# The copy of a value product's result, one slot earlier at the end of each attention layer

## The reference

```python
# layer 0: 16 query heads, 8 key/value heads of 128, RMS norm and rotation of q and k, window of 128
probs = softmax(where(mask, (q * scale) @ k.T, lowest))
x = x + einsum('btnh,nhd->btd', probs @ v, out_kernel)
x = x + sparse_2_of_4(silu(h @ w_gate) * (h @ w_up)) @ w_down    # h = layernorm(x)
# layer 1: 16 heads of 128, causal
z = softmax(masked / sqrt(128)) @ v
x = x + einsum('df,bqf->bqd', W_O, z_flat)
x = x + fwht(silu(h @ W1.T) * (h @ W3.T)) @ W2.T
```

## Time and profile before

| what | us |
|---|---|
| time, median of 3 runs | 709.01 (708.73 to 710.05) |
| the profiled execution: time | 709.12 |
| its span, first to last instruction | 707.3 |
| TensorE busy | 692.6 (98%) |
| VectorE busy | 541.0 (76%) |
| ScalarE busy | 453.3 (64%) |
| GpSimd busy | 359.5 (51%) |
| mean granted TensorE clock | 0.998 |
| layer 0, slots 60 to 63 (TensorE) | 254.44 to 264.23 |
| layer 0, slots 64 to 67 to the last output but one | 264.23 to 278.21 |
| layer 1, slots 60 to 63 | 614.81 to 623.48 |
| layer 1, slots behind 63 up to the first gate product | 623.48 to 635.78 |

### The profile page before, as it was taken

One profiled execution on the slowest core, in us unless ns is written; L12 is line 12 of the kernel. 1 busy time (PEld: TensorE's weight loads), 2 busy tenths in 40 slices (PEclk: granted clock), 3 DMA queues, 4 the chain that ended last, 5 costly groups with the idle time before them and its releaser, 6 DMA issues.

```text
span 707.3 us, 16400 instructions
## 1 busy us (share of the span) xinstructions
PE 692.6 (98%) x4540; PEld 625.4 (88%) x4540; DVE 541.0 (76%) x1696; ACT 453.3 (64%) x1794; POOL 359.5 (51%) x557
## 2 busy tenths in 40 slices
PE   6999999999999998999999999999999999999998
PEld 3789999999999997888878999999999999977887
DVE  5879999999899988969845667766767777796443
ACT  3888888888888885423257666666666666664221
POOL 5998898898899844002069842323232323016100
PEclk9999999999999999999999999999999999999999
DMA  7010210101021010100021010101001100000000
GB/s 237 2 46 9 98 46 2 46 0 44 1 104 60 0 75 2 45 1 0 16 90 61 1 61 1 61 6 54 21 38 41 63 0 0 1 1 0 1 31 31
DMA packets 9178, 24.78 MB, mean 35 GB/s; under 512 B 928, under 2 KB 3232, under 8 KB 8992
## 3 DMA queue, kind: packets, MB, share of 16 engines
q1 hardware_dynamic: 8688, 23.27, 9.7%
q10 hardware_dynamic: 432, 0.85, 0.3%
HBM read 23.07 MB, written 1.05 MB: 34 GB/s over the span
## 4 chain that ended last, share of the span: by engine, by line
PE 87%; DVE 5%; issue 3%; ACT 3%; DMA 1%; POOL 1%; SPq 0%; ACTq 0%; DVEq 0%; POOLq 0%
PE bank L508 12%; PE bank L889 11%; PE bank L500 11%; PE bank L398 11%; PE bank L527 7%; PE bank L412 5%; PE bank L366 5%; PE bank L430 5%; PE bank L359 4%; PE bank L435 3%; PE bank L963 3%; PE bank L450 3%; PE bank L967 2%; DVE x L658 1%; PE bank L983 1%
## 5 line engine op out<-in xcount | busy, mean ns | idle before, releaser
L658 DVE SCALAR_TENSOR_TENSOR x<-bank,rinv,x 128x256 f32<-128x256 f32 x256 | 123.1, 481 | 25.0 <-PE bank L398 22.8
L636 ACT ACTIVATE probs<-scores,negmax 128x128 f32<-128x128 f32 (+1 forms) x256 | 117.4, 470 | 9.3 <-DVE negmax L696 7.8
L544 ACT CAST turned<-bank 128x256 fp32r<-128x256 f32 x104 | 38.8, 373 | 101.9 <-PE bank L412 97.6
L774 POOL TENSOR_TENSOR a_hi<-raw_a,zero 128x384 fp32r<-128x384 f32 (+1 forms) x60 | 43.6, 726 | 84.6 <-PE bank L527 84.6
L669 DVE TENSOR_TENSOR enc_lo<-bank,enc_hi 128x256 fp32r<-128x256 f32 x128 | 54.2, 423 | 30.8 <-PE bank L366 21.0
L302 POOL TENSOR_TENSOR ln_r<-ln_ve,neg_half 128x1 f32<-128x1 f32 x26 | 17.0, 654 | 118.8 <-DVE ln_ve L276 118.8
L677 DVE TENSOR_TENSOR turned<-bank,turned 128x256 fp32r<-128x256 f32 x104 | 43.7, 420 | 40.4 <-ACT probs_t L545 40.4
L398 PE MATMUL bank<-b_hi,enc_hi 128*128 128x256 f32 x256 | 73.4, 287 | 0.0
L398 PE MATMUL bank<-b_lo,enc_hi 128*128 128x256 f32 x256 | 72.3, 283 | 0.0
L398 PE MATMUL bank<-b_hi,enc_lo 128*128 128x256 f32 x256 | 72.3, 282 | 0.0
L792 POOL TENSOR_TENSOR rot_a<-rot_a,rot_b 128x384 f32<-128x384 f32 x64 | 64.7, 1011 | 8.5 <-DVE rot_b L764 7.3
(11 more groups left out here) (179 smaller groups left out, 2397.3 us busy)
## 6 DMA issues: line engine op xcount, KB each, us to landing
raw_a<-in_wa SPq DMA_DIRECT2D x10, 768.0 KB, 4.4
raw_a<-in_wa SPq DMA_DIRECT2D x9, 512.0 KB, 4.0
raw_b<-in_wb SPq DMA_DIRECT2D x16, 256.0 KB, 2.7
hid_last<-in_wax SPq DMA_DIRECT2D x2, 512.0 KB, 4.5
w_a<-in_w2t SPq DMA_DIRECT2D x1, 1024.0 KB, 4.9
raw_b<-in_wdown SPq DMA_DIRECT2D x2, 512.0 KB, 3.4
x<-in_x SPq DMA_DIRECT2D x3, 256.0 KB, 4.6
raw_a<-in_wa ACTq DMA_DIRECT2D x1, 512.0 KB, 3.8
```

The lines of the kernel that those rows point to most:

```text
L636: nc.scalar.activation(probs[:, c % 4, c0:c1], scores[:, c % 2, c0:c1], ACT.Exp, bias=negmax[:, c % 2, r:r + 1], scale=-1.0, accum_out=row ...
L658: nc.vector.scalar_tensor_tensor(out=x[:, m % 8, :], in0=output_bank(m)[:, hh * D:(hh + 1) * D], scalar=rinv[:, u, r:r + 1], in1=x[:, m % ...
```

## The change

It touches three places. First, the copy `enc_hi` leaves the body of `act_slot` for a function `act_encoded(m)`. Up to slot 60 it is called as before, with m = c - 4. From slot 60 on it is called with m = c - 3, behind the copy of the turned probabilities and ahead of the exponentials; so slot 60 does both units 56 and 57, and each later one the unit whose value product TensorE does in that slot. This holds for `act_slot` in layer 0's drain too. Second, in VectorE's slots 61 to 63, the remainder `enc_lo` of unit c - 4 comes ahead of the first half of the residual, where it stood between the halves. Third, the same in `tail(t)` for t > 0 of VectorE (layer 1's slots 64 to 70). `dve_drain0` is unchanged: there the remainder was first already.

```diff
--- before.py
+++ after.py
@@ -546,18 +546,23 @@
                 else:
                     nc.scalar.copy(probs_t[:, m % 2, :], bank[PT_BANK][:, 0:384]).then_inc(s["ptev"], 1)
 
-        def act_slot(act, L, it, c):
+        def act_encoded(act, L, it, m):
+
             s = at[L]
-            if c <= TAIL_SLOT:
-                act_turned(act, L, it, c - 3)
-
-            m = c - 4
             if live(it, m):
                 u = m % 8
                 b, hh = u // 2, u % 2
                 need(act, s["pv"], it, m + 1)
                 need(act, s["op"], it, m - hh - 6)
                 nc.scalar.copy(enc[0][:, hh, b * D:(b + 1) * D], bank[O_BANK][:, 0:D]).then_inc(s["ehi"], 1)
+
+        def act_slot(act, L, it, c):
+            s = at[L]
+            if c <= TAIL_SLOT:
+                act_turned(act, L, it, c - 3)
+
+            if c <= TAIL_SLOT:
+                act_encoded(act, L, it, c - 4)
             m = c + 4
             if live(it, m):
                 t = m % 8
@@ -629,6 +634,7 @@
                 act_late_hi(act, c - UNITS + 2)
             if c >= TAIL_SLOT:
                 act_turned(act, L, it, c - 2)
+                act_encoded(act, L, it, c - 3)
             if live(it, c):
                 need(act, s["pt"], it, c - 3)
                 for r, (c0, c1) in enumerate(((0, 128), (128, 384))):
@@ -724,8 +730,11 @@
             else:
 
                 if c < UNITS:
+                    if c > TAIL_SLOT:
+                        dve_enc_lo(dve, L, it, c)
                     dve_residual(dve, L, it, c, 0)
-                    dve_enc_lo(dve, L, it, c)
+                    if c == TAIL_SLOT:
+                        dve_enc_lo(dve, L, it, c)
                     dve_heads_lo(dve, L, it, c)
                     dve_residual(dve, L, it, c, 1)
                     dve_scores_wait(dve, L, it, c)
@@ -1651,8 +1660,8 @@
                     if t < 0:
                         return
                     if t > 0:
+                        dve_enc_lo(dve, L, None, c)
                         dve_residual(dve, L, None, c, 0)
-                        dve_enc_lo(dve, L, None, c)
                         dve_residual(dve, L, None, c, 1)
                         ln_dve_scale(dve, st, t - 1)
                     dve.wait_ge(at[L]["opadd"], UNITS - 8 + t + 1)
```

## The result

The changed kernel takes 713.98 us (median of 5 runs, 712.82 to 714.29) against 709.01 us (708.73 to 710.05): ratio 1.0063, 95% interval 1.0052 to 1.0073. It is slower, by 5.0 us where 2.8 were forecast. The profiled execution took 714.29 us, its span is 712.5.

What follows compares the result with a forecast made beforehand. It took TensorE's product list plus gaps as the bound: hand-overs in layer 0's drain, nearly full VectorE in layer 1's tail. Layer 0 +1.6 and layer 1 +1.2 made +2.8 on 709.12, so 711.9 us, range 709.9 to 713.3.

Steps and rivals of the forecast that it cites:

- Gain ahead of value product 62 in layer 0: Layer 0 from slot 60: earlier copies and remainders shorten TensorE's waits, so product 62 starts 1.0 us earlier.
- First ring: Layer 0: product 62, its copy, `xT_hi` 0, `xT_lo` 0, `xn`, transposition 1 wait in turn; 2.7 us, was 1.46.
- idle time: Layer 0's drain: TensorE idle about 1.9 us ahead of transposition 1, where it was 0.65, and the same at the next.
- Layer 0 without the clock: Layer 0's net loss from both rings after the gain ahead of them: +1.6 us, with no clock effect included.
- Exponentials at no cost: Slots 60 on, both layers: ScalarE's exponentials start 0.2 to 0.9 us later, costed at nothing.
- Layer 1: Layer 1's tail: late `xT_hi` copies and VectorE's new order together cost +1.2 us, reaching TensorE in full.
- `xT_lo` 0 and 1: Layer 1's tail: these VectorE steps, waiting for late `xT_hi` copies, come 0.8 and 1.1 us later.
- VectorE's order: Residual halves side by side cost 0.13 us a slot, hidden by VectorE's idle time or waits; 0.1 in layer 1's slot 67.
- the ring: Both layers: `xT_hi` behind a copy waiting for a value product makes three engines wait in turn; both rings close, chance 0.66.
- the gain in layer 1: Layer 1, wait at 625.18: remainder of result 60 ahead of half a residual starts that value product 0.4 us earlier.
- rival (d): Layer 0's drain: gaps of about 1.9 us lower TensorE's clock, +1.0 us or more, 713.2 us; chance 0.06.
- the drain of before has gaps too and stays at 1.00: Argument against the clock falling in layer 0's drain: the kernel before has gaps there and keeps full clock.

Runs made afterwards that it cites:

- e3: Changed kernel plus eight unused matmuls in each of the two long TensorE gaps of layer 0's drain, ahead of transpositions 1 and 2; 712.73 us.
- e1: Changed kernel with ScalarE's order of before from slot 64 on, the changed one in slots 60 to 63; VectorE's order stays changed; 708.32 us.
- e6: e1 with VectorE in the order of before; 707.75 us.
- e2: Changed kernel with VectorE's three hunks undone, so only ScalarE's part of the change remains; 713.65 us.
- e8: Changed kernel with extra unused matmuls in only the second long gap of layer 0's drain, ahead of transposition 2; 712.96 us.
- e7: Changed kernel with extra unused matmuls in only the first long gap of layer 0's drain, ahead of transposition 1; 713.36 us.
- e4: Kernel before with only VectorE's part of the change; ScalarE as before; 712.87 us.
- e9: Changed kernel with VectorE's layer 0 drain reordered in slots 65 and 66: both residual halves and `xn` ahead of `xT_lo`; 710.31 us.
- e5: Kernel before with the change to ScalarE and VectorE applied only in layer 1; 710.67 us.

## Why the prediction was wrong

Up to the clock, the mechanism held step by step. Gain ahead of value product 62 in layer 0: forecast -1.0, after 267.68 - 254.59 = 13.09 from slot 60 where it was 14.04, so -0.95. First ring: transposition 1 forecast 2.7 us after product 62's start, it is 2.72; idle time forecast 1.9, it is 1.91 and 2.00. Layer 0 without the clock: forecast +1.6, e3 +1.61. Exponentials at no cost: e1 and e6 bear it out. Layer 1: forecast +1.2, measured +1.40. The sizes inside it fit too: `xT_lo` 0 and 1 are 0.86 and 1.25 us later from slot 60 than before (forecast 0.8 and 1.1), value product 62 is 0.40 earlier (forecast 0.4). How much belongs to which part depends on the order in which one adds them. From e6 (-0.51 against before), VectorE's order adds 0.97 (e1) and the ring then 0.94; the other way round the ring adds 2.07 (e2) and VectorE's order then takes 0.16 off. With the ring closed VectorE has waits that hide the order (1.24 and 0.70 us for `xT_hi` 0 and 1 in e2, 0.59 and 0.19 in the changed kernel), as the prediction said. One reason in it doesn't hold: it put the gain in layer 1 down to the remainder that moves ahead of half a residual, but e6 and e2, which leave VectorE's order alone, have value product 61 0.50 us earlier from slot 60 than before, the changed kernel 0.39.

The step that failed is rival (d), "the gaps of about 1.9 us in layer 0 slow TensorE". I gave it a chance of 0.06 and a price of 1.0 us, and the sum put the clock at nothing. It is what happened in the profiled execution, and e3 puts its price there at 2.11 us; with that, 711.9 would have become 714.0. Two things were wrong in it. The chance leant on "the drain of before has gaps too and stays at 1.00", but these gaps are 0.65 us and less, a third of those that I forecast myself; a row at 0.65 says nothing of 1.9. The price assumed that the stretch holds only 1.0 us of TensorE's work, as the window near the start does. But from 271.6 to 278.5 us stood a value product, a transposition and twelve gate and up matmuls, these at 0.41 us each for 0.28. Of the 2.11 us, 0.65 lie ahead of transposition 2, as the ring waits for the slow value product 63 (that transposition comes 20.51 us after slot 60, 19.86 in e3), and the rest behind it. With 1.6 + 2.1 + 1.4 the sum is +5.1, the span's difference 5.2. The Trainium skill's TensorE: Matmul & The Clock Gate (Part 1: The HAM clock gate) has the rule that idleness returns the array to its lower clock. The changed kernel and e8 agree, with 0.50 behind a gap of 1.91 us, and e3 with 1.00 where both gaps are filled; e7, at 1.00 over a gap of 2.00, shows that such a gap doesn't do it each time.

The clock doesn't fall the same way each time: of the changed kernel's five runs the fastest, 712.82 us, had a mean clock of 0.997, the slowest, 714.29, one of 0.992. Only the slowest has a trace, so whether the clock fell less in the fastest one's layer 0 or near its start is open. What decides between two executions, and between e8's first gap and e2's, no run here shows.

## What to carry to other kernels

A copy moved earlier in an in-order queue takes its wait along: before it is moved past a step, ask whether the engine it waits for needs that step, by way of a third engine, to get there. Here it paid in the slots with exponentials behind it and cost where a layer norm copy stood behind it, so the same edit in seven slots was two edits. And when a forecast itself makes a gap on TensorE longer than any that the trace shows, the clock belongs in the sum, priced by all the matmuls that follow the gap.

## What the runs showed of the hardware

A gap of 1.91 us halved TensorE's clock behind it in two traces (the changed kernel, e8) and not in a third (e2); at the same end of layer 0, gaps up to 1.04 us left it at 1.00 (e4, e9). In the changed kernel the mean clock of the whole execution, 0.992 for 0.998, hardly tells of it. Filling the gaps with matmuls whose results nobody reads, in time that was lost anyway, made the section 2.11 us shorter (1.25 us between the medians).

The same code takes a different time to reach slot 60 of layer 0: 254.44 us before, 256.07 in e4's trace, though nothing ahead of it was edited. In e4's trace the clock was low for longer near the start, as its windows show (the kernel before has 0.50 from 16 to 18 us too, but 0.91 on average from 18 to 22 us):

```profile
18.00:20.00 2.00, 2.00 (x7) 1.56 (x7) 1.16 (x4) 1.20 (x8) 2.00 (x3) 0.50 0.00 0
20.00:22.00 2.00, 2.00 (x7) 1.45 (x6) 0.99 (x3) 0.21 (x1) 1.83 (x4) 0.54 0.00 0
```

A spread of 1.6 us from the start alone is as large as most effects here. Single times of the kernel before lie between 708.1 and 710.8 us. Sections inside a trace repeat much better: layer 0's is 24.56 in both traces that leave it alone (before, e5), layer 1's 22.37 to 22.41 in the six traces that have the whole change there. So they tell differences of 0.1 us apart, which the times can't.
